# Expert stage of a decoder layer: the eighth output head is summed on VectorE instead of being multiplied on TensorE through a diagonal matrix

## The reference, cut to what matters

```python
scores, indices = product_key_top1(x)            # per token: 8 heads, one of 8192 experts each
A_in, B_in   = in_a[indices],  in_b[indices]     # rows of 512 and of 1024
A_out, B_out = out_a[indices], out_b[indices]    # rows of 1024 and of 512
gate   = relu(scores)
hidden = x @ W_in.T
lin    = einsum('bnd,bnhkd->bnhk', x, A_in) * gate
hidden = gelu(hidden + einsum('bnhk,bnhkd->bnd', lin, B_in))
out    = hidden @ W_out.T
lout   = einsum('bnd,bnhkd->bnhk', hidden, A_out) * gate
out    = out + einsum('bnhk,bnhkd->bnd', lout, B_out)      # sum over 8 heads
```

## Time and profile before

| | us |
|---|---|
| median of 3 runs | 2529.19 |
| lowest and highest of the runs | 2523.79, 2531.36 |
| the profiled execution, its own time | 2526.88 |
| the profiled execution, span of the trace | 2524.8 |
| busy in the span: PE, DVE, ACT, POOL | 2377.8, 2022.1, 1245.3, 1259.0 |

### The profile page before, as it was taken

How to read it: one execution, slowest core, us unless ns; L and a number is a source line. 1 busy time by engine, 2 the same in 40 slices (tenths; PEclk the granted TensorE clock), 3 DMA queues, 4 the chain that set the end, 5 groups by cost and what they waited for, 6 DMA issues and landing times. The chain is left out here.

```text
span 2524.8 us, 41365 instructions
## 1 busy us (share of the span) xinstructions
PE 2377.8 (94%) x12820; PEld 1323.0 (52%) x12820; DVE 2022.1 (80%) x5701; ACT 1245.3 (49%) x3124; POOL 1259.0 (50%) x1718
## 2 busy tenths in 40 slices
PE   7889999999999999999989799999999999999985
PEld 4456666665666665665655344444444444444432
DVE  4466777677766777667764499999999999999998
ACT  2266676666666776667666133333333333333332
POOL 1133333333333333333332367777777777777772
PEclk9999999999999999999999999999999999999998
DMA  3144555455454555445457789999999999999996
GB/s 113 45 129 129 149 154 160 123 142 164 137 154 123 149 159 159 124 141 161 135 162 248 266 334 395 393 386 387 389 389 383 393 397 389 388 387 389 386 378 273
DMA packets 292745, 622.49 MB, mean 247 GB/s; under 512 B 162352, under 2 KB 163376, under 8 KB 292528
## 3 DMA queue, kind: packets, MB, share of 16 engines
q0 software_dynamic: 83968, 438.34, 45.6%
q1 hardware_dynamic: 173760, 80.84, 12.1%
q10 hardware_dynamic: 34800, 100.68, 11.8%
HBM read 577.80 MB, written 142.61 MB: 285 GB/s over the span
## 5 line engine op out<-in xcount | busy, mean ns | idle before, releaser
L1061 ACT ACTIVATE in_rows<-scores,nmx 128x512 f32<-128x512 f32 x512 | 373.1, 729 | 116.7 <-DVE nmx L1252 113.2
L1602 PE MATMUL l_bank<-fold,xn_tf 128*128 128x512 f32 x960 | 421.6, 593 | 0.0
L1067 ACT COPY in_rows<-t_bank 128x512 f32<-128x512 f32 x512 | 298.8, 584 | 217.1 <-PE t_bank L718 216.2
L625 POOL TENSOR_TENSOR added<-mask_add,band 128x136 f32<-128x136 f32 (+1 forms) x512 | 246.8, 484 | 258.1 <-DVE nmx L1252 256.8
L1568 POOL DMA_INDIRECT in_rows<-rows_in,rows_now x248 | 296.1, 1194 | 147.2 <-DVE hid L1841 81.0
L1579 POOL DMA_INDIRECT out_rows<-rows_out,rows_now x256 | 266.4, 1041 | 136.6 <-PE out_ps L1648 54.7
L718 PE MATMUL t_bank<-ident,in_rows 128*128 128x128 f32 x2048 | 319.1, 281 | 9.8 <-ACT in_rows L1034 5.1
L718 PEld LDWEIGHTS t_bank<-ident,in_rows 128*128 128x128 f32 x2048 | 237.3, 143 | 170.9 <-issue 101.4
L686 PE MATMUL a_bank<-fold 128*128 128x256 f32 (+1 forms) x1024 | 302.8, 440 | 16.4 <-ACT fold L982 6.9
L1602 PEld LDWEIGHTS l_bank<-fold,xn_tf 128*128 128x128 f32 x960 | 182.7, 190 | 229.3 <-issue 229.3
L1850 DVE CUSTOM_DVE_ANT_0 out_rows<-out_rows,hid 128x1024 f32<-128x1024 f32 x256 | 299.7, 1216 | 2.4 <-ACT hid L1727 2.4
(11 more groups left out here) (217 smaller groups left out, 4145.6 us busy)
## 6 DMA issues: line engine op xcount, KB each, us to landing
rows_in<-in_in_b_dram ACTq DMA_DIRECT2D x16, 2048.0 KB, 8.5
rows_out<-in_out_a_dram ACTq DMA_DIRECT2D x16, 2048.0 KB, 8.9
rows_in<-in_in_a_dram ACTq DMA_DIRECT2D x16, 1024.0 KB, 8.3
rows_out<-in_out_b_dram ACTq DMA_DIRECT2D x16, 1024.0 KB, 5.6
rel_scratch<-rel_pad SPq DMA_DIRECT2D x16, 640.0 KB, 3.2
band<-rel_scratch SPq DMA_DIRECT2D x512, 20.0 KB, 2.6
prob_scratch<-in_rows SPq DMA_DIRECT2D x512, 20.0 KB, 2.0
near<-prob_scratch SPq DMA_DIRECT2D x64, 156.1 KB, 3.2
```

The lines of the kernel that those rows point to most:

```text
L625: nc.gpsimd.tensor_tensor(added[:, s % 2, lo:hi], mask[:, lo:hi], band[:, group % 2, g, lo - first:hi - first], ALU.add).then_inc(added_re ...
L1061: nc.scalar.activation(prob_tile(s % PSLOTS), scores[:, s % 2, :], ACT.Exp, bias=nmx[:, s:s + 1], scale=-1.0, accum_out=lsum[:, s:s + 1]). ...
L1067: nc.scalar.copy(prob_t[:, n // HPT % 2, n % HPT, :, :].rearrange("p k q -> p (k q)"), bank[:]).then_inc(t_emptied, 1)
L1602: ins = nc.tensor.matmul(l_bank[c % 2][:], xn_t[:, k, :], fold[:, k, c * BANK:(c + 1) * BANK], start=(k == 0), stop=(k == KD - 1))
```

## The change

Head 7 joins `VE_OUT`, which is now all eight heads. TensorE's pass with `diag_out` is gone, `dense_out` ends with its 16th pass and tells `out_filled` there. ScalarE makes no output diagonal; it gates all eight heads in a row, after its copy of the turned tokens (`take_tokens`), where the gate and the diagonal of head 7 had stood ahead of that copy. VectorE makes the products in the order 0 to 7 and one more sum, number 7, into `out_ps` (7 - `FREE_OUT` is even). GpSimd gathers in the order 0 to 7, each as its sum is done. Semaphore counts follow.

```diff
-    PE_OUT = (HEADS - 1,)
-    VE_OUT = tuple(h for h in range(HEADS) if h not in PE_OUT)
+    VE_OUT = tuple(range(HEADS))
...
-                for n, h in enumerate((*PE_OUT, *VE_OUT)):
-                    if h in PE_OUT:
-                        wait(pool, out_filled, r)
-                    else:
-                        wait(pool, out_b_used, (r - 1) * len(VE_OUT) + n - len(PE_OUT) + 1)
+                for n, h in enumerate(VE_OUT):
+                    wait(pool, out_b_used, (r - 1) * len(VE_OUT) + n + 1)
                     nc.gpsimd.indirect_dma_start(
...
                 for k in range(KF):
-                    nc.tensor.matmul(out_ps[:], hid_t[:, k, :], w_out[:, k, :], start=(k == 0), stop=False,
-                                     skip_group_check=True)
-                pe.wait_ge(diag_out_ready, r + 1)
-                for i, h in enumerate(PE_OUT):
-                    ins = nc.tensor.matmul(out_ps[:], diag_out[:, i, :], out_b[:, h, :], start=False,
-                                           stop=(h == PE_OUT[-1]), skip_group_check=True)
+                    ins = nc.tensor.matmul(out_ps[:], hid_t[:, k, :], w_out[:, k, :], start=(k == 0),
+                                           stop=(k == KF - 1), skip_group_check=True)
                 ins.then_inc(out_filled, 1)
...
             def gates_out(r):
+                wait(act, out_b_used, r * len(VE_OUT))
                 for n, h in enumerate(VE_OUT):
-                    gate_out(r, len(PE_OUT) + n, h)
+                    gate_out(r, n, h)
...
-            def diagonals_out(r):
-                wait(act, out_filled, r)
-                wait(act, out_b_used, r * len(VE_OUT))
-                for n, h in enumerate(PE_OUT):
-                    gate_out(r, n, h)
-                act.wait_ge(lout_gated, r * HEADS + len(PE_OUT))
-                for i, h in enumerate(PE_OUT):
-                    ins = nc.scalar.activation(diag_out[:, i, :], ident[:], ACT.Copy, scale=lout[:, h:h + 1])
-                ins.then_inc(diag_out_ready, 1)
...
                 take_hidden(r)
-                diagonals_out(r)
                 if not nothing_after(r, 3):
                     take_tokens(r + 3)
                 gates_out(r)
...
-                dve.wait_ge(lout_gated, r * HEADS + len(PE_OUT) + h + 1)
+                dve.wait_ge(lout_gated, r * HEADS + h + 1)
...
-                for h in (*PE_OUT, *VE_OUT[:FREE_OUT + 1]):
+                for h in VE_OUT[:FREE_OUT + 1]:
                     product_out(r, h)
```

More of the change, by code:

```diff
@@ L1457, in expert_pass @@
         diag = sb("diag", [P, len(PE_HEADS), P])
-        diag_out = sb("diag_out", [P, len(PE_OUT), P])
         hid = sb("hid", [P, F])
@@ L1481, in expert_pass @@
         lout_gated = sem("lout_gated")
-        diag_out_ready = sem("diag_out_ready")
         diag_ready = sem("diag_ready")
@@ L1731, in residual @@
                 act.wait_ge(xn_loaded[slot], 16 * filled(r, slot))
-                wait(act, out_b_used, (r - 1) * (HEADS - len(PE_OUT)) + 1 if r > 0 else 0)
+                wait(act, out_b_used, (r - 1) * HEADS + 1 if r > 0 else 0)
                 if r == 0:
@@ L1845, in product_out @@
             def product_out(r, h):
-                if h == PE_OUT[0]:
+                if h == VE_OUT[0]:
                     wait(dve, lout_gated, r * HEADS)
```

## The result

The changed kernel takes 2532.48 us (median of 17 runs, 2529.45 to 2535.44) against 2528.30 us of the kernel before (17 runs, 2522.79 to 2531.36). The ratio is 1.0019 with a 95% interval of 1.0011 to 1.0026: slower by 4.8 us (2.8 to 6.6); the two medians by themselves differ by 4.2. That is inside the forecast range, within 0.3% as forecast, and of the forecast sign; the forecast had +7.1. The profiled execution has a span of 2530.5 us, 5.7 above the one before.

A forecast was written before the change was run, and what follows sets the result against it. TensorE was taken to bound the kernel, VectorE following with 0.47 us a round to spare. Terms of +5.3 (28 rounds), +2.0 (rounds 0, 29, 30) and -0.2 (round 31) gave +7.1 on 2526.88: 2534.0 us, range 2526 to 2546.

The forecast's parts named there:

- Which engine bounds, and the turn: Expert stage: TensorE bounds before at 33.72 us a round; after the change VectorE does, at 33.91.
- The price of the sum, 0.66: VectorE's added 128x512 sum in each round costs 0.66 us, bounds 0.61 and 0.78, in the bank as in `res`.
- Its waits of 13.2 us vanish: VectorE's waits at the first `sum_in`, 0.47 us a round in 28 rounds, go, leaving 18.5 - 13.2 = +5.3 us.
- round 0 at 33.18: Round 0, where VectorE didn't wait, took 33.18 us, against 33.25 of VectorE's own work in later rounds.
- a rival: VectorE takes the added sum nearly for nothing, TensorE staying the bound: about 2505 us, half of it 2516; chance 0.05.
- Rounds 0, 29 and 30, 0.66 each: The added sum costs 0.66 us in each of these rounds, +2.0 together; VectorE's waits in 29 and 30 are no slack.
- Round 31, -0.2: Last round: TensorE is done 0.86 us earlier, then the added sum takes 0.66, so -0.2.
- What costs nothing: ScalarE's gates, GpSimd's gathers and SyncE's store stay off the path; the first output gather starts some 1.3 us earlier.
- TensorE's pauses of about 1.05 us for gelu: TensorE would wait about 1.05 us a round for gelu before it turns `hid`, from 33.91 - 32.86.
- rival 1: TensorE's clock falls in its new pauses for gelu: +34 us, so 2568; chance 0.04.
- Rival 2, the diagonal: At `heads_in` the input diagonal becomes the new wait, each 0.1 us beyond about 1.1 costing 2.8; 2545 at 0.4; chance 0.06.

The follow-up runs named there:

- e1: The changed kernel without the sum of head 7 (VectorE adds seven heads, TensorE none): 2511.90 us, ratio 0.9936 to the kernel before.
- e2: The kernel before, TensorE's pass kept, with one more sum on VectorE (head 6 added a second time): 2535.85 us, ratio 1.0033.
- e3: The kernel before, TensorE starting the product with W_out at the first half of hid_t, waiting for the second four calls later: 2513.93 us, ratio 0.9950.
- e4: The changed kernel with the wait for hid_t split in halves, the second four calls later: 2532.08 us, ratio 1.0018 to the kernel before.
- the filling: Extra TensorE calls in the pauses of the last two rounds: on the changed kernel 2530.33 us, on the kernel before with the split hid_t wait 2510.47 us.

## Why the prediction was right, point by point

- **Which engine bounds, and the turn.** Right. VectorE's waits at the first `sum_in` are gone and TensorE waits for gelu instead; e1, e2 and the pair e3 and e4 each show it from another side. A round is the larger of TensorE's need, 33.72 with its pass, and VectorE's, 33.17 and 33.81 with seven and eight sums.
- **The price of the sum, 0.66.** Right, in the bank as in `res`. The difference that the Trainium skill, "VectorE: DVE Perf Modes", gives for PSUM in its errata section is not seen between these rows; the measurement decides here.
- **"Its waits of 13.2 us vanish".** This is the term that was mis-sized. They vanished, but they were worth 0.55 a round, not 0.47, because the row counts idle time and VectorE's rows overlap; with 0.02 from the pitch behind that sum, the 28 rounds cost 2.67 us and not 5.3. The prediction had a sign of it in its hands, round 0 at 33.18, and used it only to weigh a rival.
- **Rounds 0, 29 and 30, 0.66 each.** Round 0 was right (+0.64). In rounds 29 and 30 the step was right that VectorE's waits there are no slack, but it took the length of TensorE's passes behind the pauses as given: +0.30 and +2.19. The passes of round 31 and what lies behind them to the sum are +1.53, those of round 30 -0.37. The clock sets this length, as the filling shows; why it went up in the one round and down in the other stays open.
- **Round 31, -0.2.** It was +0.22: the 16 passes of the product with `W_out` took 9.10 us instead of 8.68, behind a granted clock of 0.59 (from 2503 to 2514 us). That takes back 0.42 of the 0.86; the rest went as stated, and the clock was left out here too.
- **What costs nothing.** Right. No output product waits for a gather, the first gather starts 6.8 us after the round's first output product instead of 8.6 us. That is 1.8 earlier and not 1.3, because the row numbers ahead of it took 0.59 us instead of 1.06 (last section).
- **TensorE's pauses of about 1.05 us for gelu.** The row has 21.3 us in 28 rounds, 0.76 a round. From start to start the turning of `hid` comes 0.90 us later behind the pass ahead of it than before, so the row undercounts again; with 33.81 in place of 33.91 the forecast's own sum gives 0.95. The granted clock stayed at 1.00, so rival 1 did not come; after a pause of 10 us in the tail it did fall. What the Trainium skill, "TensorE: Matmul & The Clock Gate", says in its table on why this matters, that idle gaps between matmul bursts should be kept short, agrees with these two rows.
- **Rival 2, the diagonal.** Not in the changed kernel; with the split the wait appeared (6.0 us in 27 rounds, e4) and cost nothing, because VectorE's own work covers it.

That 7.1 came near 4.8 is in part luck: 2.6 us too much in the even rounds and some 1.6 too little in the last three, and the latter goes by the clock in one execution of each kernel. A time of this size also stands in a spread from the other stage: in the nine profiled executions of the nine kernels, the first output product of round 0 stands anywhere between 1463.02 and 1468.50 us, though nothing of the attention stage was touched. Rounds in the trace told 0.01 us apart what the medians could not.

## What to carry to other kernels

Where two engines are both full, find which one waits for the other, and give work only from the one that is waited for; here the 0.86 us a round taken off TensorE bought 0.02 once VectorE had the sum, and without the sum it brought 0.55, since VectorE's own need of 33.17 then set the pace. Measure the room of a waiting engine from start to start, against the same pair of instructions in a round without the wait, since idle time in a row leaves out the overlap. When the last rounds have less work for TensorE, look at its granted clock there: a few calls that nobody needs took 5.9 us off the tail of one kernel here and 3.4 off that of another, in the trace.

## What the runs showed of the hardware that was not expected

GpSimd's rows changed though its instructions did not: from 1510 to 2450 us the output gathers took 1.04 us on average before and 1.19 after, and the row numbers (`rows_now`) 1.06 before and 0.59 after, while the input gathers stayed at 1.20. The row numbers took 0.59 in the three runs made from the changed kernel and 1.06 in the four made from the kernel before; e1 has no eighth sum and 0.59, e2 has one and 1.06, so it is not the sum that does it. No run here was made to find the cause, and VectorE waited for no gather.
